# Language-model tower on one core: row places issued later on ScalarE, and whole-row products of q with the context

## What is computed

```
h = [pos, nest, seg embeddings] @ W                     # 16 x 256 x 128
q, k, v = split(layernorm(h) @ w_qkv.T)                 # 8 heads, chunks of 128 tokens
q', k' = exp(t @ proj.T - max)                          # 64 features a head
D   = q' . sum(k')          (+ 0.0001)
out = (q' @ (k'.T @ v)) / D                             # within the chunk of 128 tokens
h += out @ w_out.T + b_out
gates = softmax(layernorm(h) @ Wg + bg); top 2, weights normalised
h += sum over the two experts of w * (relu(x @ W1 + b1) @ W2 + b2)
```

## Time and profile before

| | |
|---|---|
| median of 3 runs | 370.96 us (367.45 to 371.57) |
| the profiled execution | 368.57 us, its span 366.8 us |
| busy share of the span | PE 91%, PEld 81%, DVE 83%, ACT 67%, POOL 53% |
| product of q and context (line 1711) | 512 instructions, 37.2 us busy |
| out projection (line 1726) | 256 instructions, 37.9 us busy |
| eight instructions of the projection in the chain | 0.95 us in most pairs; 1.81 us at 200.22 and 206.74 |
| context copies (line 868) | 32, 379 ns mean |
| row places (line 900) | 28, 293 ns mean |
| POOL's last constant | starts 7.38, 0.21 us long |
| TensorE's first embedding product | 20.97 us |
| a k product and the k maximum that takes it | 161.21 to 161.60, and 162.73 us |

### The profile page before, as it was taken

How to read it: one execution, slowest core, us unless ns; L and a number is a source line. 1 busy time by engine, 2 the same in 40 slices (tenths; PEclk the granted TensorE clock), 3 DMA queues, 4 the chain that set the end, 5 groups by cost and what they waited for, 6 DMA issues and landing times.

```text
span 366.8 us, 11920 instructions
## 1 busy us (share of the span) xinstructions
PE 334.7 (91%) x3273; PEld 296.6 (81%) x3273; DVE 303.0 (83%) x1190; ACT 244.8 (67%) x722; POOL 195.1 (53%) x345
## 2 busy tenths in 40 slices
PE   7948999999999988999997979999999999999983
PEld 3616788787787777777876879999999999999983
DVE  7585799999997888988897448889997777878986
ACT  1634777878776887778786247876776777776640
POOL 6010231766664765656765437787876545555430
PEclk9965899999999999999998569999999999999998
DMA  6084740000010000101000202223333222226767
GB/s 162 27 238 128 215 174 2 25 26 26 28 34 32 27 27 16 32 32 32 21 23 26 81 8 68 84 79 94 97 119 108 89 70 77 67 79 191 223 208 229
DMA packets 33131, 30.47 MB, mean 83 GB/s; under 512 B 4701, under 2 KB 27320, under 8 KB 33080
## 3 DMA queue, kind: packets, MB, share of 16 engines
q1 hardware_dynamic: 25848, 18.81, 17.8%
q0 software_dynamic: 4224, 9.18, 7.1%
q10 hardware_dynamic: 3008, 1.89, 1.9%
HBM read 16.42 MB, written 13.44 MB: 81 GB/s over the span
## 4 chain that ended last, share of the span: by engine, by line
PE 68%; DVE 17%; issue 8%; ACT 4%; DMA 1%; DVEq 1%; SPq 1%; ACTq 0%
PE ps_oy L1815 9%; PE ps_v L1815 9%; PE ps_out L1805 9%; PE ps_q L1805 7%; PE ps_oy L1726 6%; PE ps_out L1711 5%; PE ps_qT L1698 4%; PE ps_qT L1797 2%; PE ps_k L1805 2%; PE ps_oy L1719 2%; ACT oT L873 2%; DVE k_prime L1090 2%; DVE q_prime L1090 2%; PE ps_k L1661 2%; DVE stats L1067 1%
## 5 line engine op out<-in xcount | busy, mean ns | idle before, releaser
L776 POOL DMA_INDIRECT y_dram<-heads_out,place x68 | 69.4, 1020 | 44.2 <-ACT heads_out L966 33.4
L754 POOL DMA_INDIRECT slots_dram<-rows,row_id x64 | 63.6, 993 | 20.2 <-issue 19.4
L957 ACT ACTIVATE k_prime<-ps_out,b_T 128x128 f32<-128x128 f32 x105 | 31.1, 365 | 19.9 <-PE ps_out L1805 19.1
L728 POOL TENSOR_TENSOR rstd<-moments,ln_eps 128x4 f32<-128x4 f32 (+1 forms) x19 | 3.7, 195 | 74.9 <-DVE moments L1073 74.8
L957 ACT ACTIVATE k_prime<-ps_q,b_T 128x128 f32<-128x128 f32 x108 | 31.9, 366 | 17.2 <-PE ps_q L1805 17.0
L1815 PE MATMUL ps_oy<-w_tile,k_prime 128*128 128x128 f32 x288 | 38.3, 276 | 1.1 <-issue 1.1
L1726 PE MATMUL ps_oy<-out_w,oT 128*128 128x128 f32 x256 | 37.9, 294 | 0.0
L1815 PE MATMUL ps_v<-w_tile,k_prime 128*128 128x128 f32 x280 | 37.1, 276 | 0.4 <-issue 0.3
L1711 PE MATMUL ps_out<-context,qT 64*128 64x65 f32 x512 | 37.2, 287 | 0.0
L1805 PE MATMUL ps_out<-sT,w_tile 128*128 128x128 f32 x280 | 37.0, 275 | 0.0
L1815 PEld LDWEIGHTS ps_oy<-w_tile,k_prime 128*128 128x128 f32 x288 | 35.0, 192 | 1.6 <-issue 1.6
(11 more groups left out here) (280 smaller groups left out, 856.3 us busy)
## 6 DMA issues: line engine op xcount, KB each, us to landing
qkv_rows<-slots_dram SPq DMA_DIRECT2D x71, 72.0 KB
y_sum<-y_dram SPq DMA_DIRECT2D x14, 256.0 KB, 3.4
w_all<-in_L_ffn_W SPq DMA_DIRECT2D x1, 2048.0 KB, 13.8
w_all<-in_L_ffn_W SPq DMA_DIRECT2D x8, 256.0 KB, 4.4
out<-h SPq DMA_DIRECT2D x6, 256.0 KB, 3.7
y_dram<-heads_out,place POOLq DMA_INDIRECT x68, 2.3
y_dram<-y_sum SPq DMA_DIRECT2D x2, 512.0 KB, 4.5
slots_dram<-rows,row_id POOLq DMA_INDIRECT x64, 2.3
```

What stands on the lines that cost most here:

```text
L754: nc.gpsimd.indirect_dma_start(slots_dram[:, :], bass.IndirectOffsetOnAxis(row_id[:, place_of(p, a), j, k:k + 1], 0), rows[:, place_of(p, ...
L776: nc.gpsimd.indirect_dma_start(y_dram[:, :], bass.IndirectOffsetOnAxis(place[:, a, :], 0), y[:, a, :], None).then_inc(s_placed[a], 16)
L957: last = nc.scalar.activation(hT[:, a % 2, c, :], ps_up[a % 2][0][:, c * P:c * P + P], ACT.Relu, bias=b1_T[:, bass.ds(experts[0] * FC + c, ...
```

## The change

Three edits go together.

- On ScalarE `row_places` of a pair is issued behind the copy of the transposed q, no longer in front of oT's copy. The wait for `mask` goes with it.
- The context is kept as whole rows of the array: for each group of two heads 128 partitions x 2 x 65, the even head's context in the upper 64 partitions of the first 65 columns, the odd head's in the lower 64 of the other 65, zeros elsewhere. POOL writes the zeros once (128 x 1040 floats) and ScalarE copies the two halves by one instruction each.
- TensorE multiplies the transposed q of a group (128 rows) with 130 columns: 4 products a tile instead of 8, 8 instructions instead of 16. The two heads of a group now lie side by side in one bank, so VectorE's division writes the heads in plain order.

```diff
-        context = sb("context", [P, 2, HC, DH + 1])
+        context = sb("context", [P, 2, HC, 2, DH + 1])
...
+            nc.gpsimd.memset(context[:, :, :, :, :], 0.0).then_inc(s_ones, 1)
...
-                nc.scalar.activation(context[:, a, :, :], ps_ctx, ACT.Copy).then_inc(s_cr, 1)
+                nc.scalar.activation(context[0:DH, a, :, 0, :], ps_ctx[0:DH], ACT.Copy)
+                nc.scalar.activation(context[DH:P, a, :, 1, :], ps_ctx[DH:P], ACT.Copy).then_inc(s_cr, 1)
...
                 if live(p - 3):
                     exps_of(p - 3)
-                    row_places(p - 3, 1 - a)
                 if live(t - 1, TILES):
                     oT_copy(t - 1, 1)
                 if live(t + 1, TILES):
                     k_exp(t + 1, a, 1)
                     qT_copy(t + 1, 1)
+                if live(p - 3):
+                    row_places(p - 3, 1 - a)
...
-            act.wait_ge(s_ones, 2)
+            act.wait_ge(s_ones, 3)
...
-                    heads_out[:, a, :].rearrange("p (c r d) -> p r c d", r=2, c=HC), heads[:, :, :, 0:DH],
+                    heads_out[:, a, :].rearrange("p (r c d) -> p r c d", r=2, c=HC), heads[:, :, :, 0:DH],
...
                 for c in range(HC):
-                    for r in range(2):
-                        at = slice(DH * r, DH * r + DH)
-                        last = nc.tensor.matmul(heads[:, r, c, :], qT[at, a, c, :], context[at, a, c, :], start=False,
-                                                stop=(c == HC - 1), skip_group_check=True)
+                    at = c % 2 * 2 * (DH + 1)
+                    last = nc.tensor.matmul(ps_out[:, c // 2, at:at + 2 * (DH + 1)], qT[:, a, c, :],
+                                            context[:, a, c, :, :].rearrange("p r d -> p (r d)"), start=False,
+                                            stop=(c % 2 == 1), skip_group_check=True)
```

## The result

The changed kernel takes **352.78 us** (median of 4 runs, 352.55 to 354.0) against 370.18 us of the kernel before in the same session (4 runs, 367.45 to 371.57): ratio 0.9545, 95% interval 0.9483 to 0.9607 (a ratio, here and below, leaves disturbed executions out, so it can differ a little from the quotient of the medians). The prediction was 360.3 us with a range of 355.5 to 364.5: the direction is right, the gain of 17.4 us is larger than the range allowed. The profiled execution took 354.0 us, its span is 352.2 us; before, 368.57 and 366.8. So 14.6 us can be followed from trace to trace; the other 2.8 lie between those executions and the medians.

A forecast was written before the change was run, and what follows sets the result against it. Attention pairs were held by a chain of waits from VectorE's mask through ScalarE's oT copy to TensorE; gains of 11.15 us less 0.6 gave 10.6, from 368.57 to 358.0 profiled, 360.3 us median, range 355.5 to 364.5.

The forecast's parts named there:

- part 1: Pairs with choices: row places behind q's copy let oT's copy go early; 0.9 us a loop pair, 0.70 an unrolled one.
- the gain is its idle time: Pairs: VectorE becomes the bound, so its idle time is gained; 0.97 us a loop pair, 0.9 taken; 0.70 unrolled.
- The 0.6 us off for ends that meet: Deduction from the summed gain of 11.15 us, for ends that meet within 0.1 us, leaving 10.6.
- the pair with the loop's table change: Middle of attention: this pair gains 0.16 us, plus 0.6 from three tiles of whole-row products.
- part 2: Eight whole-row products for sixteen half-row ones: 0.19 us a tile, bounds 0 and 0.23, only where TensorE bounds.
- the 0.11 to 0.15 on leaving: TensorE, instruction behind the products: half-row products may cost the next one 0.11 to 0.15 us, which would go.
- part 3: ScalarE, two context copies for one: 0.27 to 0.38 us more a tile, off the path; 0.05 a pair charged.
- part 4: POOL zeroes the context once near 4 us: about 1 us, hidden by setup.
- Rival (b): End of attention: TensorE's clock doesn't fall, work of 200 to 209 us some 4 us shorter, 356.3 us; chance 0.17.
- The median: Whole run: median of the runs 2.4 us above the profiled execution, so 360.4 against 358.0.
- as long as now: Expert stage, 216 to 350 us: TensorE busy end to end, untouched by the change, so it only shifts.
- Rival (c): Pairs: early oT copy gains nothing because rank products wait for the same mask; about 2 us, 369; chance 0.05.

The follow-up runs named there:

- e1: Kernel before with only the row places moved behind the copy of the transposed q, half-row products kept: 358.77 us against 369.93.
- e10: Changed kernel with its whole-row products made per head, sixteen of 128 rows and 65 columns a tile: 377.36 us against 368.84 of the kernel before.
- e11: Changed kernel plus 32 products of zeros on TensorE, at the start, ahead of the last rank products and ahead of the experts: 348.89 us.
- e12: Kernel before with the row places moved and 32 products of zeros added, half-row products and single context copy kept: 348.82 us against 369.39.
- e9: Kernel before plus 15 products of zeros in TensorE's idle times at the start: 362.12 us against 368.84.
- e3: Kernel before plus nine products of zeros in TensorE's idle times of setup: 370.59 us against 369.93.
- e8: Kernel before plus one unused VectorE sum of 128 x 256 elements a pair: 371.64 us against 370.95, ratio 1.0002.
- e5: Kernel before with eight products in one half of the array, then eight in the other, instead of alternating: 379.75 us against 370.95.
- e2: Changed kernel with the row places back in their old place, so whole rows, two context copies and zeros alone: 364.6 us against 369.93.
- e4: Changed kernel plus 17 products of zeros, nine in setup and eight ahead of the last rank products: 352.72 us against 369.93 of the kernel before.
- e6: Changed kernel plus one more unused ScalarE copy of half a context a tile: 356.97 us against 370.95 of the kernel before.
- e7: Changed kernel plus one unused VectorE sum of 128 x 256 elements a pair: 356.18 us against 370.95 of the kernel before.

## Why the prediction was right or wrong

**The move (part 1): the mechanism right, the size too small.** Every step of it is in the trace: the copy ahead of the mask, the projection directly behind the rank products, VectorE as the new bound. The term of 0.9 us a loop pair measured 1.11, the 0.70 an unrolled pair 0.92, and e1 shows 1.01 and 0.90 for the move alone. The step that failed is "the gain is its idle time". VectorE's idle time in a loop pair went from 1.19 us (11.16 - 9.97) to 0.29 (10.05 - 66.02 x 10.05 / 68.00 = 10.05 - 9.76), and that is the 0.9 that was forecast. The other 0.21 us is busy time: 9.97 against 9.76 us, for the same 40 instructions a pair. They overlap. In the kernel before, k's maximum starts 0.87 us behind the start of the row numbers' reduction (167.05 to 167.92), in the kernel after 0.11 (145.68 to 145.79), before the 0.16 us of the reduction are over: 0.76 us from this one wait, whose idle time says 0.69. The distance from start to start between two instructions is the number to subtract, not the idle time alone.

**The 0.6 us off for ends that meet** were not needed: TensorE and VectorE are both full and cost each other nothing that can be seen. As much was put in for whole rows where that did not help: the pair with the loop's table change (106.83 to 119.33 us before) was to gain 0.16 + 0.6 us and went from 12.50 to 12.34, 0.16. So the 2.1 us by which the pairs' 10.6 exceed the 8.5 are the unrolled pairs (4 x 0.22) and those of the loop (6 x 0.2).

**Whole rows (part 2): too large, and priced by columns, which does not hold (e10).** I expected 0.19 us a tile where TensorE bounds; e11 against e12 gives 0.12, and 0.6 us ahead of the first mask. The products themselves give 0.04 to 0.06 of it (0.98 to 1.00 against 1.04 from start to start), and the 0.11 to 0.15 on leaving come only in part: the transposes directly behind go from 0.59 to 0.44, those behind the embedding product from 0.44 to 0.52. In the pairs the difference between e1 and the changed kernel is 1.3 us, between e12 and e11 1.0, and without the waits for a scatter 0.5 each. In the total nothing is left (e11 and e12).

**Context copies (part 3): right on the path, too small in time.** The second copy starts 0.39 us behind the first, above the 0.27 to 0.38 I gave. ScalarE's work is 61.84 x 10.05 / 68.00 = 9.14 us a pair, where 9.15 was forecast. **Zeroing (part 4)** left no trace in any wait.

**The clock: the step that is missing, and the largest part of the miss in the spans.** The sum took every tile and the whole tail at the pace of the kernel before. The start gave 2.9 us instead of 1.0, the tail 3.85 instead of 1.05; together 4.7 of surplus. Of the 2.9 at the start whole rows themselves account for 0.6 (e11 against e12). At the start the clock was full from 33 us on instead of from 39. First three stretches of the kernel before, the last of them its tail:

```profile
33.00:34.00 1.00, 1.00 (x12) 0.90 (x10) 0.35 (x1) 0.51 (x1) 0.00 (x0) 0.50 0.13 49
...
39.00:40.00 1.00, 1.00 (x18) 0.94 (x18) 0.64 (x2) 1.00 (x3) 0.00 (x0) 0.99 0.98 290
...
198.00:217.00 19.00, 14.86 (x96) 13.65 (x96) 8.49 (x43) 7.29 (x24) 10.05 (x23) 0.55 0.14 40
```

And the tail of the kernel after:

```profile
184.00:200.00 16.00, 11.20 (x88) 10.30 (x88) 9.17 (x45) 7.19 (x24) 10.05 (x23) 0.80 0.16 48
```

In the tail the mean is 0.80 instead of 0.55. The 0.72 us for oT are gone, as forecast, and the 1.75 us for the mask stay (1.96 now); the clock is at 0.50 in 187 to 188 us, at 0.95 in 190 to 192, at 1.00 to 194 and low again from about 197, where it had stayed low from 199.4 to 216. Rival (b), worked out at 4 us and given 0.17, was half of the story: it happened in part, 2.8 us, and had a twin at the start that no rival named. The profile of before held both dips, in slices 3 to 5 and 22 to 24 of its clock line; I made a rival of the second, and of the first I used only that one tile runs at half clock. e9 and e11 show that the clock is a lever by itself (6.7 and 3.9 us), and e12 that the move and the clock together are the whole gain.

**The median.** I put it 2.4 us above the profiled execution, as it stood before. After, it is 1.2 us below. The offset goes at least in part with the clock: single executions of the kernel before take 367.0 us at a mean clock of 0.96 and 371.5 to 372 at 0.942, and the profiled one, with the clock up at 39 us, was one of the luckier (its mean clock of 0.949 alone does not say so); e3 and e8, with the rise at 43 to 44, have their first mask at 66.2 instead of 64.06. The runs of the changed kernel agree within 1.5 us. These 3.6 us and the 4.0 of the spans make up the miss of 7.5.

**The experts: forecast "as long as now", measured 2.8 us longer.** VectorE waits 2.0 us there for the write of the heads' sums and TensorE 1.0 us for the read of the slots (waits from 204 to 350 us), and the kernel before has no such waits there:

```profile
DVE slot_w L1478 <- DMA y_dram<-heads_out,place: 2.0, 2, 1.2
...
PE ps_qT L1800 <- DMA qkv_rows<-slots_dram: 1.0, 1, 1.0
```

The timeline says where the time went:

```profile
216.99 0.15 DVE L1478 COPY slot_w<-qkv_rows 128x1 f32 x1 [1.20 <-DMA y_dram<-heads_out,place]
...
265.50 0.33 PE L1800 MATMUL ps_qT<-ident,qkv_rows 128*128 128x128 f32 x1 [0.97 <-DMA qkv_rows<-slots_dram]
```

At these two places the transposes of successive slot tiles are 3.07 and 3.03 us apart, where the kernel before has 2.11 and 1.90: 2.1 of the 2.8 us. Between them and behind them the pace is the same; from the 41st slot tile to the 71st both kernels take 56.9 us. The rest is 0.2 us ahead of them, 0.3 behind the last slot tile, and 0.2 in steps next to the two. So the experts' work is no slower, two transfers land late.

Why they do is **open**. In single traces this stage takes 149.3 to 150.7 us in the seven kernels with half-row products (before, e1, e3, e5, e8, e9, e12), and 150.8 to 152.2 in six with eight whole-row products (after, e2, e4, e6, e7, e11), but 149.7 in e10, which has whole rows and sixteen products; and e8, with half-row products, has such a wait too (0.35 us at 286.0). No experiment was made on it. Open too is **why** the clock rises at 33 to 36 us with eight products of 130 columns and at 39 to 48 us with sixteen of 65: TensorE is busy all the time in both (1.00 of 1.00 in 33 to 34 us, in both traces), and in e1 it is busy 9.00 of 9.00 us from 36 to 45 at half clock.

**Rival (c)** is out: the wait for k is gone, and with e1 alone.

## What to carry to other kernels

Before pricing a change, read the line of the granted clock and price its dips as a stage of their own: here two dips of 17 us each cost about as much as the whole rescheduling of sixteen pairs brought (of the 19.7 us between the spans of before and e12, 9.6 lie in the pairs, 4.2 ahead of them and 5.8 behind, the latter with the 0.7 us of oT's wait), and 32 products of zeros closed them. Take the gain of a removed wait from the distance between the starts of two instructions of the next bound, not from the idle time alone: instructions that follow each other without a wait overlap. And price a change of one engine's instructions by the length of a whole tile in which that engine bounds, not by two groups of it. Then test who is the bound by adding a little work to each engine before and after. A small instruction behind somebody else's result (here 0.49 us of row places behind a mask) costs what is queued behind it, so order an in-order queue by when the inputs are there.

## What the runs showed of the hardware

- Fp32 products that alternate between the upper and the lower 64 rows of the array, and between two banks, ran at 65 ns each (65 columns); in the same half and bank one after the other at 96 ns (e5); over 128 rows at 113 ns with 65 columns (e10) and 122 to 125 ns with 130 (after), from start to start. Halving the columns saved about 10 ns.
- Four transposes directly behind half-row products took 0.59 us in the chain, behind whole-row ones 0.44. A whole tile gained less than that: 9.17 against 8.94 us for two, product included (e12, e11).
- A ScalarE copy of 64 partitions x 260 elements takes 0.37 to 0.39 us, one of 128 partitions 0.37: halving the partitions saves nothing.
- Products of zeros where TensorE had idled 0.75 to 2.62 us kept the granted clock at 1.00 all through the start (e9, e11, e12), though TensorE was busy only 1.38 of 3.00 us in 24 to 27 us of e9 and e11; 9 of them instead of 15 moved the fall from 22 us to 27 us in the trace of e3, and its median gained nothing.
- In the start of these kernels the clock stayed at half for 10.2 us with eight instructions of 130 columns a tile (four traces) and for 17.1 to 23.9 us with sixteen of 65 (six traces).
- A scatter can land late: one took 4.46 us in e1's chain, where the median on its profile page is 2.3 us, and held ScalarE up for 0.86 us; that pair is 0.77 us longer than the others.
